# The residual sum of each scan step moved from VectorE to GpSimd, by way of a copy that ScalarE makes

## The reference

```python
x = x + scan_block(ctx_1024, z=layernorm(x))      # in_proj 256->512, causal convolution of 4 taps, SiLU -> u
#   x_dbl = x_proj(u) -> dt_low, B, C;  dt = softplus(dt_proj(dt_low) + bias);  A = -exp(A_log)
#   state = state * exp(dt * A) + (dt * u) * B;   y = sum over states of state * C;   y = (y + D * u) * silu(z)
x = x + layernorm(x) @ (sum of 8 factors) / sqrt(8) + bias
```

## Time and profile before

| | us |
|---|---|
| median of 3 runs | 547.08 (546.94 to 547.17) |
| the profiled execution | 552.13 |
| its span, first to last instruction | 550.3 |
| VectorE busy | 480.7 (87%) |
| GpSimd busy | 440.9 (80%) |
| TensorE busy | 430.8 (78%) |
| ScalarE busy | 348.3 (63%) |

### The profile page before, as it was taken

How to read it: one execution, slowest core, us unless ns; L and a number is a source line. 1 busy time by engine, 2 the same in 40 slices (tenths; PEclk the granted TensorE clock), 3 DMA queues, 4 the chain that set the end, 5 groups by cost and what they waited for, 6 DMA issues and landing times.

```text
span 550.3 us, 3951 instructions
## 1 busy us (share of the span) xinstructions
PE 430.8 (78%) x988; PEld 179.0 (33%) x1000; DVE 480.7 (87%) x390; ACT 348.3 (63%) x607; POOL 440.9 (80%) x219
## 2 busy tenths in 40 slices
PE   7626868786868678878978788958898788888797
PEld 4202323322323233323433233423333233333343
DVE  5699899988999899986999899974999899999642
ACT  2575754847466976858676876756676967565240
POOL 1047999999989989985999989975999899999200
PEclk9875978898887879988999899889999999989999
DMA  5999355447871000100591000000591000000012
GB/s 168 271 247 391 127 77 114 76 76 155 306 243 65 0 0 1 57 1 1 191 412 51 0 19 1 21 0 0 170 413 72 0 19 1 20 0 19 0 40 76
DMA packets 20287, 53.69 MB, mean 98 GB/s; under 512 B 2708, under 2 KB 2708, under 8 KB 20264
## 3 DMA queue, kind: packets, MB, share of 16 engines
q1 hardware_dynamic: 16296, 45.05, 22.7%
q0 software_dynamic: 3968, 8.39, 8.5%
HBM read 48.98 MB, written 4.46 MB: 97 GB/s over the span
## 4 chain that ended last, share of the span: by engine, by line
DVE 41%; issue 19%; PE 18%; ACT 9%; POOL 8%; DMA 3%; SPq 1%; DVEq 0%; ACTq 0%; POOLq 0%
DVE dA L719 20%; DVE h L719 9%; DVE h L725 7%; PE y L356 6%; POOL h L850 5%; PE work L349 4%; PE work L316 3%; ACT dA L552 3%; DVE acc L667 2%; POOL h L843 2%; PE work L437 2%; DMA b_rep<-bc_scratch 2%; ACT gate L470 1%; DVE work L707 1%; DVE work L701 1%
## 5 line engine op out<-in xcount | busy, mean ns | idle before, releaser
L356 PE MATMUL y<-h,ident 128*128 128x512 f32 x512 | 266.5, 657 | 78.1 <-DVE h L725 72.4
L850 POOL TENSOR_TENSOR h<-b_rep,dtu 128x1024 f32<-128x1024 f32 x127 | 306.4, 2478 | 11.1 <-DMA b_rep<-bc_scratch 10.7
L552 ACT ACTIVATE dA<-dt,a_neg 128x512 f32<-128x512 f32 x256 | 165.6, 679 | 95.2 <-DVE h L725 73.6
L719 DVE TENSOR_TENSOR_SCAN dA<-dA,h 128x1024 f32<-128x1024 f32 x80 | 182.8, 2285 | 28.1 <-ACT dA L552 26.8
L356 PEld LDWEIGHTS y<-h,ident 128*128 128x128 f32 x512 | 99.8, 205 | 227.3 <-DVE h L725 111.2
L843 POOL TENSOR_TENSOR h<-h,c_rep 128x1024 f32<-128x1024 f32 x48 | 117.9, 2456 | 33.8 <-DVE h L719 33.8
L719 DVE TENSOR_TENSOR_SCAN h<-dA,h 128x1024 f32<-128x1024 f32 x48 | 109.4, 2279 | 3.5 <-ACT dA L552 2.9
L725 DVE TENSOR_TENSOR h<-dA,c_rep 128x1024 f32<-128x1024 f32 x80 | 97.1, 1214 | 1.2 <-DVE dA L719 0.3
L349 PE MATMUL work<-fsum,xnT 128*128 128x512 f32 x88 | 41.9, 621 | 0.0
L308 PE MATMUL work<-ctx_sb,w_in 128*128 128x512 f32 x60 | 29.9, 628 | 14.5 <-DVE x L739 13.2
L667 DVE SCALAR_TENSOR_TENSOR acc<-work,chan,acc 128x511 f32<-128x511 f32 (+2 forms) x45 | 32.2, 728 | 0.2
(11 more groups left out here) (111 smaller groups left out, 366.9 us busy)
## 6 DMA issues: line engine op xcount, KB each, us to landing
b_rep<-bc_scratch SPq DMA_DIRECT2D x32, 512.0 KB, 7.9
c_rep<-bc_scratch SPq DMA_DIRECT2D x32, 512.0 KB, 8.3
fsum<-factors POOLq DMA_DIRECT2D x8, 1024.0 KB, 9.1
x<-x SPq DMA_DIRECT2D x4, 1024.0 KB, 8.2
out<-x SPq DMA_DIRECT2D x16, 256.0 KB, 2.0
ctx_sb<-ctxT SPq DMA_DIRECT2D x3, 512.0 KB, 5.8
ctx_sb<-ctxT SPq DMA_DIRECT2D x2, 256.0 KB, 4.2
w_in<-w_inT SPq DMA_DIRECT2D x2, 256.0 KB, 4.5
```

The lines of the kernel that those rows point to most:

```text
L356: mm = pe.matmul(y[:], ident[:], h[:, (s * PAIRS + j) % H_RING, i, :], start=False, stop=(j == SUM_ORDER[-1] and i == 1))
L552: act.activation(dA[:, j % 2, i, :], dt[:, k % 2, :], ACT.Exp, scale=a_neg[:, k, 2 * j + i:2 * j + i + 1]).then_inc(exp_done, 1)
L719: dve.tensor_tensor_scan(pair if j in POOL_C else decay, decay, pair, 0.0, ALU.mult, ALU.add).then_inc(scanned, 1)
L850: pool.tensor_tensor(h[:, (s * PAIRS + j) % H_RING], b_rep[:, j], dtu[:, k % 2, :].unsqueeze(1).to_broadcast([P, 2, L]), ALU.mult).then_in ...
```

## The change

The fifteen sums inside the steps move to GpSimd. GpSimd adds from a new tile `yT`, which ScalarE fills with a copy of `work0`. On ScalarE the copy comes at j = 3 after the decays; on GpSimd the sum comes at j = 6 after the fill. TensorE's projection into `work0` now waits for the copy. The sum after the last step stays on VectorE as it was.

```diff
@@ -102,6 +102,7 @@
         h = sb("h", [P, H_RING, 2, L])
 
         yg = sb("yg", [P, L])
+        yT = sb("yT", [P, L])
         xn = sb("xn", [P, DI])
         xnT = sb("xnT", [P, KB, P])
         bias_row = xn
@@ -163,6 +164,7 @@
         gated = sem("gated")
         y_turned = sem("y_turned")
         x1_added = sem("x1_added")
+        yT_copied = sem("yT_copied")
         t_mean, t_var, t_lnv, t_expv, t_nb, t_xn, t_turned, t_xnT, t_ffn, t_final = (
             sem(f"t_{n}") for n in ("mean", "var", "lnv", "expv", "nb", "xn", "turned", "xnT", "ffn", "final"))
 
@@ -378,7 +380,7 @@
                     if i == 1 and nu < STEPS:
                         pe.wait_ge(ctx_landed, nu // KB * 16)
                         if s > 0:
-                            pe.wait_ge(x1_added, s)
+                            pe.wait_ge(yT_copied, s)
                         else:
                             pe.wait_ge(conv, conv_count(KB))
                         in_proj(work0, nu % KB)
@@ -461,6 +463,12 @@
                     act.wait_ge(d_dtu, (b - 1) * KB)
                 act.activation(u[:, b % 2], acc[:], ACT.Silu).then_inc(u_done, KB)
 
+            def yT_copy(s):
+                act.wait_ge(y_turned, s + 1)
+                if s > 0:
+                    act.wait_ge(x1_added, s)
+                act.activation(yT[:], work0[:], ACT.Copy).then_inc(yT_copied, 1)
+
             def gate_batch(b):
 
                 act.wait_ge(g_nb, b + 1)
@@ -583,6 +591,8 @@
                     if j == 2:
                         if nt >= 2:
                             t_final_(nt - 2)
+                    if j == 3 and s > 0:
+                        yT_copy(s - 1)
                     if j == 2 and is_g:
                         act.wait_ge(x_landed, (b + 2) * 16)
                         act.wait_ge(g_nb, b + 1)
@@ -750,8 +760,6 @@
                         conv_part(work0, nv - 1, 3)
                     if j == 1 and s > 0:
                         gate_y(s - 1)
-                    if j == 3 and s > 0:
-                        add_x1(s - 1)
                     if j == 2 and is_d:
                         softplus_poly(s + 1)
                         softplus_sum(s + 1)
@@ -837,6 +845,13 @@
                 pool.wait_ge(d_dtu, n + 1)
                 pool.memset(dt[:, k % 2, 0:1], RESET).then_inc(dt_reset, 1)
 
+            def add_x1(s):
+                b, k = divmod(s, KB)
+                pool.wait_ge(yT_copied, s + 1)
+                pool.wait_ge(g_done, (b + 1) * KB)
+                pool.tensor_tensor(x1_columns(b, k), yT[:].rearrange("p (t d) -> p t d", t=KB),
+                                   x1_columns(b, k), ALU.add).then_inc(x1_added, 1)
+
             def times_c(p):
                 pool.wait_ge(scanned, p + 1)
                 pool.wait_ge(c_landed[p % PAIRS], (p // (KB * PAIRS) + 1) * 16)
@@ -870,6 +885,8 @@
                         times_b(b, s, k, j)
                     if p >= C_LAG and on_pool(p - C_LAG):
                         times_c(p - C_LAG)
+                    if j == 6 and s > 0:
+                        add_x1(s - 1)
                 if s + 1 < STEPS:
                     dt_times_u(s + 1, (k + 1) % KB)
```

## The result

The change makes the kernel slower: 565.24 us (median of 4 runs, 564.1 to 566.24) against 547.12 (4 runs, 546.94 to 555.65), a ratio of 1.031 with a 95% interval of 1.026 to 1.036. I had forecast 558.2 with a range of 547 to 563. The sign was right and so was the engine, GpSimd; the size was not (18.1 us were lost where 11.1 were forecast), nor the place where most of it is lost.

A forecast was written before the change was run, and what follows sets the result against it. VectorE and GpSimd were taken as both nearly full inside the scan steps, so GpSimd's lateness decides. 7.2 up to step 12, 2.1 in the last steps and 1.8 for TensorE's clock gave +11.1: 558.2 us, range 547 to 563.

The forecast's parts named there:

- the hand-overs: Steps 4, 8, 12: ScalarE's mean pass waits for the batch's adds; main term, +1.06 each even without GpSimd lateness.
- VectorE's saving: The add leaving VectorE gains 0.59 us in each step where VectorE sets the pace.
- A rule against the change: VectorE's two-SBUF-input g_r product excludes GpSimd's SBUF reads; steps 3, 7, 11 held longer, 0 to +2 in all, taken as 0.
- but it is: At steps 4, 8, 12, GpSimd's C product of pair 0 itself starts late, 2.09 us in step 4.
- my 7.2 up to step 12: Accumulated delay at the decays of pair 5 in step 12, 430.49 against 423.29: +7.2 us.
- c0(8): GpSimd's C product of pair 0 in step 8, forecast to start at 289.87.
- The add (1.28): GpSimd's new add in each step, priced at 1.28 us from the two-input product L836.
- the copy (0.60): ScalarE's new copy out of PSUM, priced from L548; costs its 0.60 us only in steps 2, 6 and 10.
- The last steps (+3.9): Steps 13 to 15: GpSimd's late C product delays the last sums, +2.1, and TensorE's low clock adds 1.8.
- The median: The runs' median, 547.08, lay 5 us below the profiled execution's 552.13; the same +11.1 was added to it.
- The rival of contention: VectorE's scans and products meet the added GpSimd reads, each add holding VectorE 1.28: up to 19 us more, 577; chance 0.04.

## Why the prediction was wrong

The forecast was 7.0 us short. In the profiled executions the change cost 13.4 us where I had 11.1, which is 2.3 of it; the other 4.7 are the 5 us that I took off for the median. The 2.3 hide larger errors: the holds took 7.1 where I had nothing, the hand-overs 3.3 where I had 7.3 (both net of VectorE's saving), 1.5 isn't the change's, and TensorE's clock gave back 2.0.

- **The g_r product ("A rule against the change", 0 to +2, taken as 0)** is the step that failed. I had read from 878 against 151 ns that it is held, and then priced the hold by one fill at most and let GpSimd's own lateness hide it. It was the other way round: the hold came first and made up GpSimd's lateness, so that "but it is" late, said of the C product of pair 0 at the hand-overs, was wrong too (1.76, 1.72 and 0.72 of idle time). The product took 7.2 us more in the three steps than before (4.61 + 2.32 + 2.96 against 2.03 + 0.35 + 0.35). The size went wrong because the hold didn't end with the instruction that GpSimd was at: in these runs it lasted through the dt·u product unless GpSimd had waited just ahead of its C product, and with an added instruction GpSimd no longer waited there. The kernel without the add has both cases: with 0.54 us idle ahead of that C product in step 7 the g_r product took 0.37, with none in step 11 it took 1.70. The Trainium skill, page "SBUF — State Buffer", section "Who interferes with whom", has such a pair of instructions exclude one another, the second waiting for the first; the trace agrees that it waits (2.32 to 4.61 us for four columns), but the measured waits run over up to three instructions, and the measurement decides.
- **The two prices don't add up.** With the product's hold the hand-overs lost 4.7 us from pair 4 to pair 6, without it 8.9; my 7.2 up to step 12 belongs to a kernel without the hold. In that kernel (563.6 against 553.1, both with the product on ScalarE) the sum was right within 1 us, and in its profile c0(8) and the decays of pair 5 within 0.3. The sum is in part luck: between the two profiles the steps 6 and 10 gave back 1.1 us, through TensorE's clock, where I had added 1.2, and VectorE saved 0.8 less in the steps 3, 5, 7, 9 and 11 than I had counted.
- **VectorE's saving of 0.59** measured 0.45. Before, the add started 0.10 before the scan's end and the C product 0.08 before the add's end; now the C product, which needs the scan's result, starts 0.03 after the scan's end. The row was right and its neighbour the wrong one to measure by.
- **The add (1.28) and the copy (0.60)** measured 1.29 and 0.58, 0.52 of it in the steps 6 and 10.
- **The last steps (+3.9)** measured +3.2 from the start of step 13; the wait of TensorE for the last C product (4.28, forecast 4.7) and its low clock behind it (the last twelve matmuls 7.11 us at a mean of 0.76) came as forecast.
- **The median.** I carried 5 us between profile and median over to the changed kernel. They were TensorE's low clock in the steps 6 and 10 of one execution, and the changed kernel's profile isn't above its median by more than 0.3 (565.57 and 565.24). In the number this is the larger error.
- **The rival of contention** had the right kind of loss on the wrong instructions: scans (2.28 to 2.29 us in both kernels) and VectorE's C products (1.21 and 1.22) were not held, only the g_r product was.

What stays open: why one execution is granted the high clock after an idle time after which another isn't (3.72 us idle ahead of the sum of pair 5 in step 6 was followed by a sum of 1.98 in the changed kernel and of 3.78 with the product on ScalarE), and why the hold ends where it does.

## What to carry to other kernels

When work moves to an engine that is nearly full, look not for its busy share but for the places where another engine waits for it or is kept out by it; here the same fifteen adds cost 16 us at one place (565.2 against 549.2 without them) and 2 to 3 at another, 4.7 us earlier in the step and with the held product out of the way (551.1 and 552.2). If two such places follow one another, undo them together: each alone seemed worth 2 to 3 us, both were worth 12. Before a forecast is carried over to the median of the runs, a second profile of the kernel before is worth having: its two executions differed by 5 us. And a VectorE instruction of four columns, with both inputs in SBUF, beside a GpSimd that no longer pauses, can cost more than all the work that was to be saved (7.1 us against 4.9 here).

## What the runs showed of the hardware

- A VectorE product with two inputs in SBUF was held up to 4.61 us, over three GpSimd instructions in a row, and only 0.35 to 0.37 where GpSimd had just been idle for 0.27 to 0.93 us; why such a pause decides how long the hold is, no run here shows. The same product as four `tensor_scalar` with a per-partition scalar from SBUF took 0.2 us each. Scans and C products of VectorE, with one input in PSUM, were not lengthened (scans 2.28 to 2.29 us, C products 1.21 and 1.22, before and after).
- After 2.1 to 3.8 us of idle time TensorE was sometimes granted 1.00 of its clock for the next sum (1.98 us) and sometimes 0.50 (3.78 us) or a mean between; two executions of the kernel before differed by 6 us in the steps 6 and 10, where their clocks differed (0.50 to 0.79 against 1.00 in step 10). Its runs spread over 9 us; how much of that is the clock is not shown.
